# Moving norm, pooling and attention instructions within the full step of a fused conv and attention kernel

## The chip, the cores and the metric

The kernel runs on one core of one Trainium2 chip. The metric is the device time of one execution in microseconds (us). A core has five engines that run their own instruction queues strictly in program order and meet only at semaphores: TensorE (PE, matmuls into PSUM), VectorE (DVE), ScalarE (ACT), GpSimd (POOL, here mostly the issuer of DMAs that add in memory) and SyncE (SP, loads and stores).

## The reference

Eight images of 256 channels and 32x32 pixels pass through two residual blocks, each behind a group norm. The first is a pooling and convolution block, the second attention over the 1024 pixels.

```python
x = x + conv_block(_gn(x))
x = x + attention(_gn(x))

# conv_block: the stem, two chains of three 5x5 poolings each, four products
x_aux = silu(conv1x1(x, w_sta))
for _ in range(3):
    y1.append(0.9 * maxpool5(y1[-1]) + 0.1 * sumpool5(y1[-1]) / 25)   # the mixture
    y2.append(sumpool5(exp(y2[-1]) * y2[-1]) / (sumpool5(exp(y2[-1])) + 1e-6))
y = concat(silu(cv1(concat(y1))), silu(cv2(concat(y2))))       # 512 channels
a = c1(four depthwise 3-tap convolutions of y)
out = silu(cvend(y * a))

# attention: q = f w1, softmax(q f / 16) (f w2), without a key projection
```

## The kernel before

**Stages.** Phase a computes the stem, phase b the second pooling chain (`y2`) of all images into DRAM. Phase c, where the change lies, runs from 277 us to the end. It pipelines two images: step i does the convolution block of image i, the attention of image i-1, and the first pooling chain (`y1`, called "the chain") of image i+1. Steps 1 to 6 do all three (the full step; 1 to 5 are a hardware loop, which also loads for image i+2), step 0 has no attention, step 7 no chain, step 8 attention alone. The order on each engine is written out by hand in one function `step` for each engine, and nothing reorders it.

**Split products.** Each fp32 operand of a product is split in a high part (rounded, by ACT) and a low part (the rest, by DVE), and a product is three matmul passes: high by high, weights' low by high, weights' high by low. `product_split` walks the four 128-channel tiles k: tiles 0 to 2 in all three passes, then tile 3 in all three. Each output tile is 12 pairs of 512-column matmuls. The product cv1 takes the levels 0 to 3 of the chain; the last tile is level 3, the output of the third mixture. So of the first output tile of cv1, 9 pairs need levels 0 to 2 alone, pairs 10 and 11 need level 3's high part (`level_split_hi(act, i, LEVELS)`, L327) and pair 12 its low part (`level_split_lo(dve, i, LEVELS)`, L331).

**The chain.** Each level needs seven maxima on DVE (`maxima`, L309) and box sums made by eight DMA rounds (`add_round`), issued by POOL one after the other, each waiting for the one before. `mixture` (L318) joins both on DVE. `level_mixture(0)` stands in the attention's tile 2, `level_mixture(1)` behind the attention's last tile, and the third mixture (`mixture_of_added(dve, i, LEVELS - 1)`, output `last`) at the head of the next step. A mixture releases the DMA rounds of the next level.

**The norm of the attention.** At the end of a step DVE adds the block's output to x and takes statistics (`add_l0`, `bn_aggr`). At the head of the next step PE averages the means over groups in the middle of cv2's second output tile (L1313, `means`), DVE makes three small operations (L1602 to L1606), PE averages again (`variances`, between cv2 and cv1), DVE adds epsilon (L1616), POOL takes the power (L1173), DVE makes the shift (L1620), and ACT normalises (L1441) and splits (L1444).

**The head of a step.** ACT: high part of level 3, SiLU of the two cv2 tiles (L1384), centre taps 0 and 1 (L1391), the normalisation, further taps, SiLU of the cv1 tiles, then the products for q and v. DVE: outer taps (`outer_taps`, L1535, two instructions each, after their centre tap), `normalised_lo` (L1564), the low parts of q (L1650) and v (L1653). PE: cv2, variances, cv1, q products, v products, then the scores. `claim` makes PE wait until the PSUM slot of three uses ago is read.

**The attention tiles.** For each of eight query tiles t: PE score(t+1), turn_back(t-2), mix(t-1), turn(t) (a transpose of the exponentials); ACT the exponential (L1400), `turned_hi` (L1405), `scale_mixed` (L1419); DVE `turned_lo` (L1539), an outer tap, `maximum` (L1544), a piece of the chain, `invert`, `add_attention` (L1553). `inputs_lo` (L1560) follows. `released` gives the slots' conditions.

Of the kernel before, what the change touches and what calls it, by code (L numbers as in the profile page):

```python
# [38 lines left out]
KT = C4 // P  # L39
LEVELS = 3  # L40
# [946 lines left out]
MIX_AT = 2  # L987
# [6 lines left out]
def phase_c(nc, x, out, keep, levels, chain, pooled):  # L994

    with ExitStack() as ctx:
# [381 lines left out]
        def _(act):  # L1378
            def step(i, conv, attn, chained, ahead):
# [39 lines left out]
                    nc.scalar.activation(mixed[:, t % 2], ps_o[:, 0:C], ACT.Copy, scale=row_inv[:, t:t + 1]).then_inc(mixed_done.sem, 1)  # L1419

                slots_of = slot_plan(conv, attn)
                if conv and attn:
                    chain.level_split_hi(act, i, LEVELS)
                if conv and not attn:
                    for n, (c, s) in enumerate(schedule(attn)):
                        if s == 0:
                            silu_cv(c)
                        centre_tap(n)
                        if n == 1:
                            chain.begin_twos(act, i + 1, 1)  # L1430
                        if s == STAGES - 1 and c:
                            inputs_hi(c - 1)
                elif conv:
                    for n in range(CT):
                        silu_cv(n)
                    for n in range(CT):
                        centre_tap(n)
                if attn:
                    for t in range(CT):
                        wait(act, norm, i - 1, 6)  # L1440
                        nc.scalar.activation(a[:, t], x1[:, t], ACT.Identity, scale=rstd[:, t:t + 1],  # L1441
                                             bias=shift[:, t:t + 1]).then_inc(f_done.sem, 1)
                        wait(act, f_done, i - 1, t + 1)
                        nc.scalar.copy(f_hi[:, t], a[:, t]).then_inc(f_hi_done.sem, 1)  # L1444
# [19 lines left out]
                if attn:  # L1464
                    if conv:
                        centre_tap(BEFORE)
                    for t in range(TILES):
                        if t > 1:
                            scale_mixed(t - 2)
                        if t:  # L1470
                            turned_hi(t - 1)
                        if t == 1 and conv:
                            centre_tap(BEFORE + 1)
                        exponent(t)
                        if chained and t == MIX_AT + 1:
                            chain.begin_twos(act, i + 1, 1)
                        if t == TILES - 1:
                            turned_hi(t)
                        if conv and t and BEFORE + t + 1 < KT * STAGES:
                            centre_tap(BEFORE + t + 1)  # L1480
                    if conv:
                        inputs_hi(0)
                        inputs_hi(1)
                    scale_mixed(TILES - 2)
                    if conv:
                        inputs_hi(2)
                    scale_mixed(TILES - 1)
# [31 lines left out]
        def _(dve):  # L1519
            def step(i, conv, attn, chained, ahead):  # L1520
# [65 lines left out]
                def level_maxima(level, *at):  # L1586
                    chain.maxima(dve, i + 1, level, *at)
# [7 lines left out]
                before = iter(range(BEFORE if attn else KT * STAGES))  # L1595
                if conv and attn:
                    chain.level_split_lo(dve, i, LEVELS - 1)
                    chain.mixture_of_added(dve, i, LEVELS - 1)
                if attn:
                    small = Steps(dve, norm, i - 1)  # L1600
                    wait(dve, group_mean, i - 1, 1)
# [5 lines left out]
                if chained and not attn:  # L1607
                    chain.maxima(dve, i + 1, 0, first=chain.inner_ahead())
                if conv and attn:
                    chain.level_split_lo(dve, i, LEVELS)  # L1610
                elif conv:
                    outer_taps(next(before))
                    level_mixture(0)
# [8 lines left out]
                    outer_taps(next(before))  # L1622
                if conv and attn:
                    outer_taps(next(before))
                if attn:
                    for t in range(CT):
                        normalised_lo(t)
                        if conv:
                            outer_taps(next(before))
# [13 lines left out]
                if attn:  # L1643
# [14 lines left out]
                    for t in range(TILES):  # L1658
# [5 lines left out]
                            outer_taps(BEFORE + t)  # L1664
                        if t + 1 < TILES:
                            maximum(t + 1)
                        if chained and t == MIX_AT:
                            level_mixture(0)
                            level_maxima(1, 0, 1)
                        if chained and t > MIX_AT:  # L1670
                            level_maxima(1, t - MIX_AT + 1)
                        invert(t)
                        if t > 1:
                            add_attention(t - 2)
                    turned_lo(TILES - 1)
                    if conv:
                        for n in range(KT):
                            inputs_lo(n)
                if attn:
                    add_attention(TILES - 2)  # L1680
                if chained and not attn:
# [17 lines left out]
                else:  # L1699
# [28 lines left out]
                    if chained:  # L1728
# [2 lines left out]
                        level_maxima(2, 3, 4)  # L1731
                        for n in range(1, KT):
                            pooled.split_lo(dve, i + 1, n)
                        level_maxima(2, 5, 6)
                    if conv:
                        add_l0(0)
                if conv:
# [3 lines left out]
                    for m in range(CT):  # L1741
                        nc.vector.bn_aggr(mv[:, m, :], stats[:, m].rearrange("p h s -> p (h s)")).then_inc(bn.sem, 1)
                if chained:
                    chain.level_split_lo(dve, i + 1, 1)

            for n in range(KT):
# [44 lines left out]
```

## Time and profile before

| | |
|---|---|
| median of 3 runs | 1395.18 us (1388.47 to 1396.79) |
| the profiled execution | 1393.83 us, of which the span is 1391.9 us |
| PE, DVE, ACT, POOL busy | 87%, 83%, 52%, 22% of the span |
| instructions | 17764, 6702 of them matmuls |
| mean granted TensorE clock | 0.949 of full speed |
| DMA | 164.23 MB, 118 GB/s on average |

A share of the span is an average over phases with different limits. No engine is full, so the question at each stage is what its last wait was for. In the profile's chain of work that ended last, PE has 22% of the span, DVE 18%, DMA 16%, ACT 6%, and 17% is issue time without any shown wait.

### The profile page before, as it was taken

How to read it: one execution, taken by the hardware profiler on the slowest of the kernel's cores; microseconds unless marked ns; L12 is line 12 of the kernel's file. 1: busy time of each engine (PE TensorE's matmuls, PEld its weight loads, DVE VectorE, ACT ScalarE, POOL GpSimd, SP SyncE). 2: the span in 40 equal slices, each digit the busy share in tenths (PEclk: the TensorE clock that was granted, in tenths of full speed). 3: DMA queues.
4: the chain of work that ended last, by engine and by line, in shares of the span. 5: the costliest groups of instructions: out<-in, count | busy, mean ns of one | idle time of the engine just before them, and what ended most of it. 6: DMA issues, size and time to landing. Idle time of an engine off the chain costs nothing.

```text
span 1391.9 us, 17764 instructions
## 1 busy us (share of the span) xinstructions
PE 1213.2 (87%) x6702; PEld 1026.9 (74%) x6702; DVE 1154.5 (83%) x1220; ACT 723.2 (52%) x780; POOL 300.9 (22%) x256
## 2 busy tenths in 40 slices
PE   3569898675989999998999899999998999899697
PEld 1249898653768877877887788778887888788597
DVE  7779897599989989988998899889988986985443
ACT  1246766554366437634753566357545643754343
POOL 1567767501111111111111111111111111000000
PEclk9769998786999999999999999999999999999899
DMA  7403214544664576466646655764575457001000
GB/s 284 166 31 92 91 77 155 158 112 90 155 142 85 139 191 143 96 153 174 127 97 172 159 107 124 198 133 96 126 202 128 86 124 202 14 1 61 0 1 31
DMA packets 73310, 164.23 MB, mean 118 GB/s; under 512 B 33200, under 2 KB 35888, under 8 KB 73264
## 3 DMA queue, kind: packets, MB, share of 16 engines
q0 software_dynamic: 25200, 97.11, 31.1%
q1 hardware_dynamic: 47360, 66.20, 14.5%
q8 instruction: 31, 0.51, 0.2%
q10 hardware_dynamic: 704, 0.30, 0.1%
q14 instruction: 15, 0.12, 0.0%
HBM read 40.80 MB, written 25.17 MB: 47 GB/s over the span
## 4 chain that ended last, share of the span: by engine, by line
PE 22%; DVE 18%; issue 17%; DMA 16%; ACT 6%; DVEq 0%; POOL 0%; POOLq 0%; ACTq 0%
PE slot L1277 10%; DMA boxes<-twos 8%; PE ps_level L1277 8%; DMA twos<-boxes 5%; DVE between L1535 4%; DVE a L1535 4%; PE slot L1293 2%; DMA twos<-middle 2%; DVE pt_all L1539 2%; PE slot L1224 2%; ACT a L1441 1%; ACT between L1391 1%; DVE middle L318 1%; ACT y L1384 1%; DVE c_minus_max L1544 1%
## 5 line engine op out<-in xcount | busy, mean ns | idle before, releaser
L1277 PE MATMUL ps_level<-v_all,pt_all 128*128 128x256 f32 x1536 | 199.0, 286 | 13.0 <-DVE pt_all L1539 10.9
L1277 PEld LDWEIGHTS ps_level<-v_all,pt_all 128*128 128x128 f32 x1536 | 188.2, 191 | 18.3 <-DVE pt_all L1539 16.9
L1277 PE MATMUL slot<-f_all,q_all 128*128 128x512 f32 x768 | 189.7, 397 | 0.0
L1535 DVE SCALAR_TENSOR_TENSOR a<-between,k_columns,a 128x992 f32<-128x992 f32 (+1 forms) x128 | 157.6, 1232 | 6.9 <-ACT a L1391 4.6
L1277 PEld LDWEIGHTS slot<-f_all,q_all 128*128 128x128 f32 x768 | 140.1, 188 | 27.9
L1539 DVE TENSOR_TENSOR pt_all<-slot,pt_all 128x1024 fp32r<-128x1024 f32 x64 | 78.0, 1218 | 38.5 <-ACT pt_all L1405 38.2
L1419 ACT ACTIVATE mixed<-ps_level,row_inv 128x256 f32<-128x256 f32 x64 | 30.2, 472 | 133.9 <-PE ps_level L1277 133.9
L1391 ACT ACTIVATE a<-between,k_columns 128x1024 f32<-128x1024 f32 x64 | 79.3, 1239 | 33.6 <-DVE between L1535 32.6
L1414 ACT CAST v_all<-y 128x1024 fp32r<-128x1024 f32 x32 | 33.7, 1054 | 115.5 <-DVE y L1568 115.2
L1535 DVE SCALAR_TENSOR_TENSOR between<-y,k_columns,between 128x992 f32<-128x992 f32 x64 | 78.8, 1250 | 7.3 <-ACT between L1391 6.2
L1568 DVE SCALAR_TENSOR_TENSOR y<-slot,k_columns,y 128x1024 f32<-128x1024 f32 x32 | 40.9, 1283 | 52.2 <-PE slot L1224 50.6
L1405 ACT CAST pt_all<-slot 128x1024 fp32r<-128x1024 f32 x64 | 65.0, 1016 | 36.2 <-PE slot L1293 35.3
L1544 DVE TENSOR_REDUCE c_minus_max<-slot 128x1 f32<-128x1024 f32 x64 | 78.0, 1219 | 6.0 <-PE slot L1277 5.6
L1400 ACT ACTIVATE pooled<-slot,c_minus_max 128x1024 f32<-128x1024 f32 x64 | 71.6, 1119 | 21.8 <-DVE c_minus_max L1544 21.8
L1535 DVE SCALAR_TENSOR_TENSOR between<-a,k_columns,between 128x960 f32<-128x960 f32 x64 | 77.2, 1215 | 1.1
L1293 PE MATMUL slot<-k_ident,pooled 128*128 128x128 f32 x512 | 67.2, 274 | 10.2 <-ACT pooled L1400 10.2
L1224 PE MATMUL slot<-q_all,k_cv_hi 128*128 128x512 f32 x192 | 61.7, 425 | 12.0 <-ACT q_all L387 12.0
L853 POOL TENSOR_TENSOR e_lo<-x_all,e_hi 128x1024 fp32r<-128x1024 f32 x24 | 62.1, 2587 | 45.3 <-ACT e_hi L808 45.3
L1293 PEld LDWEIGHTS slot<-k_ident,pooled 128*128 128x128 f32 x512 | 56.8, 141 | 14.1 <-ACT pooled L1400 14.1
L1224 PE MATMUL slot<-f_all,k_c_hi 128*128 128x512 f32 x232 | 64.6, 400 | 0.4 <-DVE y L1568 0.4
L1224 PE MATMUL slot<-f_all,k_c_lo 128*128 128x512 f32 x232 | 63.5, 396 | 0.0
L1224 PE MATMUL slot<-q_all,k_c_hi 128*128 128x512 f32 x232 | 63.5, 395 | 0.0
(198 smaller groups left out, 2762.5 us busy)
## 6 DMA issues: line engine op xcount, KB each, us to landing
levels<-x_all SPq DMA_DIRECT2D x32, 512.0 KB, 2.6
boxes<-twos POOLq DMA_DIRECT2D x28, 543.0 KB, 4.7
boxes<-twos POOLq DMA_DIRECT2D x28, 527.0 KB, 4.6
x_all<-in_x SPq DMA_DIRECT2D x8, 1024.0 KB, 12.8
f_all<-levels SPq DMA_DIRECT2D x8, 1024.0 KB, 7.7
x<-in_x SPq DMA_DIRECT2D x8, 1024.0 KB, 6.1
out<-x SPq DMA_DIRECT2D x8, 1024.0 KB, 6.0
twos<-boxes POOLq DMA_DIRECT2D x14, 561.0 KB, 4.3
```

Source lines behind the costliest of these rows:

```text
L853: nc.gpsimd.tensor_tensor(e_lo[:, u], e[u], e_hi[:, u].bitcast(F32), ALU.subtract).then_inc(e_lo_done, 1)
L1224: last = nc.tensor.matmul(slot[:, hs], weights[:, k], inputs(k)[:, hs], start=(at == 0), stop=(at == len(uses) - 1))
L1277: last = nc.tensor.matmul(out, lhs, rhs, start=(n == 0), stop=(n == len(parts) - 1))
L1293: last = nc.tensor.transpose(slot[:, cols(m)], prob[:, cols(m)], keep["ident"][:, :])
L1391: nc.scalar.activation(dst, src, ACT.Identity, scale=keep["taps"][:, s, c, 1:2], bias=keep["b_taps"][:, s, c:c + 1]).then_inc(taps_centre. ...
L1400: nc.scalar.activation(prob[:, :], slots_of["s", t][:, :], ACT.Exp, bias=minus_max[:, t:t + 1], accum_out=row_sum[:, t:t + 1]).then_inc(pr ...
L1405: nc.scalar.copy(pt_hi[:, t % 2], slots_of["t", t][:, :]).then_inc(pt_hi_done.sem, 1)
L1414: nc.scalar.copy(y_hi[:, m], y[:, m]).then_inc(y_hi_done.sem, 1)
L1535: nc.vector.scalar_tensor_tensor(o, u, keep["taps"][:, s, c, tap:tap + 1], o, ALU.mult, ALU.add).then_inc(taps.sem, 1)
L1539: nc.vector.tensor_tensor(pt_lo[:, t % 2], slots_of["t", t][:, :], pt_hi[:, t % 2].bitcast(F32), ALU.subtract).then_inc(pt_lo_done.sem, 1)
L1544: nc.vector.tensor_reduce(minus_max[:, t:t + 1], slots_of["s", t][:, :], AX, ALU.max, negate=True).then_inc(maxed.sem, 1)
L1568: nc.vector.scalar_tensor_tensor(y[:, m], slots_of["c1", m][:, :], keep["b_c1"][:, m:m + 1], y[:, m], ALU.add, ALU.mult).then_inc(gated.se ...
```

## The change

Five pieces move, four of them in steps with attention and convolution; no instruction is added or removed.

1. DVE, head of the step: the third mixture goes behind norm's first three small operations; the low part of level 3 goes from there to behind the outer taps 0 and 1.
2. ACT, head of the step: the high part of level 3 goes behind the SiLU of both cv2 tiles and the centre taps 0 and 1.
3. ACT, attention's tile 7: its exponential goes ahead of `turned_hi(6)`. This holds for step 8 too.
4. DVE, attention's tiles: `invert` and `add_attention` go ahead of the chain's piece, and the last maximum of level 1 goes from tile 7 to between the third and the fourth `inputs_lo`.
5. DVE, tail of the step: the last two maxima of level 2 go behind the additions to x and the statistics.

```diff
@@ ScalarE
                 slots_of = slot_plan(conv, attn)
-                if conv and attn:
-                    chain.level_split_hi(act, i, LEVELS)
...
                     for n in range(CT):
                         centre_tap(n)
+                    chain.level_split_hi(act, i, LEVELS)
...
                             scale_mixed(t - 2)
+                        if t == TILES - 1:
+                            exponent(t)
                         if t:
                             turned_hi(t - 1)
...
-                        exponent(t)
+                        if t < TILES - 1:
+                            exponent(t)
@@ VectorE
                     chain.level_split_lo(dve, i, LEVELS - 1)
-                    chain.mixture_of_added(dve, i, LEVELS - 1)
...
                 if conv and attn:
-                    chain.level_split_lo(dve, i, LEVELS)
+                    chain.mixture_of_added(dve, i, LEVELS - 1)
...
                 if conv and attn:
                     outer_taps(next(before))
+                    chain.level_split_lo(dve, i, LEVELS)
...
+                        invert(t)
+                        if t > 1:
+                            add_attention(t - 2)
                         if chained and t == MIX_AT:
                             level_mixture(0)
                             level_maxima(1, 0, 1)
-                        if chained and t > MIX_AT:
+                        if chained and MIX_AT < t < TILES - 1:
                             level_maxima(1, t - MIX_AT + 1)
-                        invert(t)
-                        if t > 1:
-                            add_attention(t - 2)
                     turned_lo(TILES - 1)
                     if conv:
-                        for n in range(KT):
+                        for n in range(KT - 1):
                             inputs_lo(n)
+                    if chained:
+                        level_maxima(1, TILES - MIX_AT)
+                    if conv:
+                        inputs_lo(KT - 1)
...
-                        level_maxima(2, 5, 6)
...
                 if chained:
+                    if attn:
+                        level_maxima(2, 5, 6)
                     chain.level_split_lo(dve, i + 1, 1)
```

On VectorE at the head of the full step, before. L331 is a low part of a level, L318 the third mixture, L1602 to L1620 the norm, L1535 an outer tap; L95 and L81 prepare waits.

```order
L331 TENSOR_TENSOR pt_all<-middle,v_all 128x1024
L95 REGISTER_ALU
L81 ISA
L318 SCALAR_TENSOR_TENSOR last<-boxes,work_b 128x1024
L81 REGISTER_ALU
L1602 TENSOR_TENSOR c_dev<-c_mv,ps_level 128x2
L81 ISA
L1604 TENSOR_TENSOR c_dev<-c_dev 128x2
L81 REGISTER_ALU
L1606 TENSOR_TENSOR c_spread<-c_dev,c_mv 128x2
L95 REGISTER_ALU
L331 TENSOR_TENSOR pt_all<-last,v_all 128x1024
```

The same place after the change, from the third mixture on (the three small operations stand just ahead of it; L1537 is the outer tap's new line number).

```order
L318 SCALAR_TENSOR_TENSOR last<-boxes,work_b 128x1024
L81 REGISTER_ALU
L1617 TENSOR_SCALAR c_spread<-ps_level 128x2
L1618 TENSOR_SCALAR gmean<-ps_level 128x2
L81 REGISTER_ALU
L1621 TENSOR_TENSOR c_shift<-gmean,c_rstd 128x2
L95 ISA
L1537 SCALAR_TENSOR_TENSOR between<-y,k_columns,between 128x32x31
...
L331 TENSOR_TENSOR pt_all<-last,v_all 128x1024
L95 ISA
L1566 TENSOR_TENSOR f_all<-a,f_all 128x1024
```

Four outer-tap instructions (two outer taps, the last three replaced by the line of dots) now stand between the third mixture and level 3's low part, where there was none.

On ScalarE at the head of the full step, as one piece of the difference: L1384 is the SiLU of a cv2 tile, L1391 a centre tap, L327 the high part of level 3.

```order
+L1384 ACTIVATE y<-slot,k_columns 128x1024
+L95 REGISTER_ALU
+L1384 ACTIVATE y<-slot,k_columns 128x1024
+L1391 ACTIVATE between<-y,k_columns 128x1024 x2
+L95 ISA
 L327 CAST v_all<-last 128x1024
```

The four instructions that followed the high part of level 3 now precede it.

## Rows read from the trace of the kernel before

**Rows 1.** Chain of waits of 640 to 800 us: start us, us, what.

```profile
745.24 1.15 DVE middle L318
...
783.99 4.61 DMA boxes<-twos
...
788.73 1.24 DVE last L318
```

**Rows 2.** Timeline of DVE at the head of step 3: start us, us, instruction [idle before].

```profile
655.39 1.22 DVE L318 SCALAR_TENSOR_TENSOR last<-boxes,work_b 128x1024 f32<-128x1024 f32 x1 [1.66 <-DMA boxes<-twos]
...
660.87 4.99 DVE L1535 SCALAR_TENSOR_TENSOR between<-y,k_columns,between 128x992 f32<-128x992 f32 x4 [0.79 <-ACT between L1391]
665.78 1.22 DVE L1564 TENSOR_TENSOR f_all<-a,f_all 128x1024 fp32r<-128x1024 f32 x1
```

**Rows 3.** Timeline of ACT and of POOL at the same place.

```profile
659.61 2.37 ACT L1391 ACTIVATE between<-y,k_columns 128x1024 f32<-128x1024 f32 x2
...
656.67 0.55 POOL L214 DMA_DIRECT2D ahead_boxes<-ahead  x1
659.11 0.71 POOL L1173 TENSOR_TENSOR c_rstd<-c_spread,k_minus_half 128x2 f32<-128x2 f32 x1 [1.89 <-DVE gmean L1617]
```

**Rows 4.** Timeline of PE at the head of step 3, variances to the first score.

```profile
657.25 0.49 PE L1313 MATMUL ps_level<-c_spread,k_group 128*128 128x2 f32 x2 [2.87 <-DVE c_spread L1606]
...
664.72 0.63 PE L1224 MATMUL slot<-q_all,k_cv_hi 128*128 128x512 f32 x2
...
670.32 0.63 PE L1277 MATMUL slot<-f_all,k_w_hi 128*128 128x512 f32 x2
...
676.09 0.70 PE L1277 MATMUL slot<-k_w_hi,f_all 128*128 128x256 f32 x4
...
679.67 0.74 PE L1277 MATMUL slot<-k_w_hi,f_all 128*128 128x256 f32 x4 [0.55 <-DVE q_all L1650]
...
682.59 5.65 PE L1277 MATMUL slot<-f_all,q_all 128*128 128x512 f32 x24
```

**Rows 5.** Stretches of PE: length, busy (matmuls), granted clock, DMA share, GB/s.

```profile
657.60:661.92 4.32, 4.32 (x13) 0.63 0.73 258
332.13:337.20 5.07, 5.06 (x12) 0.56 0.55 106
343.96:348.13 4.17, 4.17 (x12) 0.66 0.00 0
```

**Rows 6.** Timeline of PE in step 0, two longer gaps.

```profile
332.13 2.93 PE L1264 MATMUL slot<-f_all,k_c_hi 128*128 128x512 f32 x6 [4.62 <-ACT f_all L1410]
...
343.96 2.93 PE L1264 MATMUL slot<-f_all,k_c_hi 128*128 128x512 f32 x6 [4.13 <-ACT f_all L1410]
```

**Rows 7.** Timeline of all engines in attention's tile 7 of step 3.

```profile
731.50 1.12 ACT L1400 ACTIVATE pooled<-slot,c_minus_max 128x1024 f32<-128x1024 f32 x1
731.63 1.23 DVE L1539 TENSOR_TENSOR pt_all<-slot,pt_all 128x1024 fp32r<-128x1024 f32 x1 [0.46 <-ACT pt_all L1405]
...
732.76 1.09 PE L1293 MATMUL slot<-k_ident,pooled 128*128 128x128 f32 x8 [1.03 <-ACT pooled L1400]
...
736.68 1.22 DVE L1539 TENSOR_TENSOR pt_all<-slot,pt_all 128x1024 fp32r<-128x1024 f32 x1
...
737.95 0.39 PE L1277 MATMUL ps_level<-v_all,pt_all 128*128 128x256 f32 x1 [1.24 <-DVE pt_all L1539]
```

**Rows 8.** Timeline of all engines, third mixture to first score in steps 1 and 7.

```profile
389.10 1.23 DVE L318 SCALAR_TENSOR_TENSOR last<-boxes,work_b 128x1024 f32<-128x1024 f32 x1 [0.58 <-DMA boxes<-twos]
...
391.19 0.28 PE L1313 MATMUL ps_level<-c_spread,k_group 128*128 128x2 f32 x2
...
416.33 0.86 PE L1277 MATMUL slot<-f_all,q_all 128*128 128x512 f32 x3
...
1186.45 1.22 DVE L318 SCALAR_TENSOR_TENSOR last<-boxes,work_b 128x1024 f32<-128x1024 f32 x1
...
1213.65 0.63 PE L1277 MATMUL slot<-f_all,q_all 128*128 128x512 f32 x2
```

## The prediction

> **What bounds the kernel now.** I read the chain of waits first. In steps 1 to 6 it runs through the third mixture, the DMA rounds of level 2 are the last thing before it, and they start from `level_mixture(1)`: 745.24 to 788.73 is 43.5 us, all DMA rounds and their issue [rows 1]. The mixtures stand 133.1 to 133.3 us apart, so the other 89.8 us (655.39 to 745.24) lead from one third mixture through the attention to `level_mixture(1)` [rows 1, 2]. Call the third mixture's start M. Nothing that merely happens earlier before M shortens a step, since M waits for the DMA (DVE idled 1.66 us for it) [rows 2]. Only work between M and `level_mixture(1)` counts.
>
> The timelines of each engine show what lies there. PE starts the first score at M + 27.20 in step 3 [rows 2, 4], and at M + 27.23 and M + 27.20 in steps 1 and 7, where PE's own waits and clock were different [rows 8]. A constant on such different PE timelines says that DVE set it: mixture, norm, outer taps, low parts of f and q, without a gap over 0.8 us. PE waited for DVE's q_lo (0.55 us) [rows 4]. From the first score on, DVE is busy without a gap until the tile-2 mixture is done, then PE is, until tile 7.
>
> **The change, part by part.** All times are those of step 3.
>
> Norm ahead of the mixture. DVE's three small operations go into its idle 1.66 us, the variances no longer wait, and PE's gap of 2.87 us with the slow stretch behind it goes [rows 4, 5]. ACT, freed of its wait for M, has SiLU and centre taps done before 657.2: two taps take 2.37 [rows 3], and cv2 ended before 654.4. Behind M (655.39 to 656.6) DVE adds epsilon; POOL is issuing DMAs until 657.22 and then takes the power, 0.71 [rows 3]; the shift ends at about 658.2, and the outer taps start at 658.3, not 660.87: 2.5 us earlier.
>
> The low part of level 3 is what this costs. It now follows those taps: 658.3 + 4.9 [rows 2] + 1.2 = 664.4, that is M + 9.0. Before, it ended at 658.9. PE starts cv1 2.8 us earlier, at 654.8, and has 11 of the first tile's 12 pairs to do before it needs that low part: 22 matmuls at 5.60/24 = 0.233 us (664.72 to 670.32 are 24) [rows 4] are 5.1 us, so it stands idle from 659.9 to 664.4, 4.5 us. The high part is ready in time (ACT at 657.9, needed at 659.0). PE's gap has moved and grown from 2.9 to 4.5 us.
>
> The clock. After the gap of 2.87 us 12 matmuls took 4.32 us at granted clocks down to 1.2 GHz, instead of 12 x 0.233 = 2.80: a loss of 1.5 us [rows 4, 5]. After gaps of 4.62 and 4.13 us, 12 took 5.07 and 4.17, losses of 2.3 and 1.4 [rows 5, 6]. The new gap is as long as these, so I take the fall for granted, at the 1.5 us of the same place, with 1.4 and 2.3 as ends.
>
> The Trainium skill (TensorE: Matmul & The Clock Gate, section Terms) puts the penalty at the throttled time times one minus the clock's ratio, half of it here. By that, the 4.32 us at a mean of 0.63 would lose 1.6 us, and the sum below would be 0.7 us larger over seven steps; the trace agrees within its rounding [rows 5].
>
> First score, new. 664.4, then 2 matmuls of cv1's first tile and 24 of the second (6.1), the clock's loss (1.5), 24 for q (5.6), two v products at 2.9 (679.67 to 682.59) [rows 4], 5.8: 683.4 = M + 28.0. DVE, 2 us ahead, no longer makes PE wait for f_lo or q_lo. Against 27.2 that is 0.8 us later: the bound passes from DVE to PE.
>
> Attention's tiles. In tile 2 the same DVE work lies before `turned_lo(2)` in either order, so PE's wait there stays. From tile 3 on PE sets the pace. In tile 7 the exponential starts at 730.6 instead of 731.50, and turn(7) about 0.9 earlier than 732.76 [rows 7]. But `turned_hi(6)` now follows it, and `turned_lo(6)` slips from 731.63 to about 732.7. Behind that DVE has an outer tap (2.4), `invert` and an addition (0.4); it no longer has a maximum (1.1). So `turned_lo(7)` starts at 732.7 + 1.1 + 2.4 + 0.4 = 736.6, where it started before, 736.68 [rows 7], and the last mix at 737.9 as before, 737.95. Gain: zero, given back within the tile. The maximum moved out fills DVE's 1.3 us wait ahead of the fourth `inputs_lo`, so it costs nothing; if that cover were gone, 1.1 us a step.
>
> Tail of the step. Statistics come 2.4 us earlier and PE's 0.9 us wait for the means goes. All of it is ahead of M: zero. DVE reaches the mixture at 654.4, still before the DMA (655.3). No queue gets a DMA earlier that could collide: the SP loads and the DMA rounds hang on c1, M and the mixtures, and shift with them. `level_mixture(0)` comes 0.6 us later, under the 4.4 us that level 1's DMA rounds have in hand before `level_mixture(1)`.
>
> **The sum.** Steps 2 to 6: 5 x 0.8 = 4.0. Step 1: PE's variances were late anyway, at 391.19 [rows 8], so SiLU, taps and low part end at 399.7; 399.7 + 6.1 + 1.5 + 5.6 + 5.8 = 418.7 against 416.33: 2.4. Step 7: DVE came to its mixture with no wait, so the small operations push M by 0.6 (1187.05), but POOL is free; low part at 1195.7, score at 1214.7 against 1213.65 [rows 8]: 1.0. In step 7's tile 7 no maximum leaves, so the slip of `turned_lo(6)` costs about 0.5, and in step 8, with nothing beside it, about 0.4 (estimates from the 0.9 to 1.0 slip, half of it covered by the earlier transpose). Together 8.3 us. The profiled execution takes 1393.83 us, which becomes 1402.1; the median of the three is 1.35 above it, and on that basis the forecast is **1403.5 us**, 0.6% slower. About 1% (14 us) is what a measurement of this kernel can tell from no change.
>
> **Rivals.**
> 1. The clock does not fall in the new gap, since PE is busy before it. For: gaps of 1.1 to 2.0 us show no fall. Against: 2.6 to 2.9 us did, in all of steps 2 to 6. It would take 7 x 1.5 = 10.5 off: 1393.0.
> 2. Slower by more: the clock falls early in the gap and stays low after it, as behind the 4.62 us gap, where the loss was 2.3 [rows 5, 6]. 7 x 0.8 = 5.6 more: 1409.1, just at the 1% bound. It decides from a slow stretch over 4.5 us behind the gap. For: the gap begins sooner, so the clock may already be down when work returns. Against: after 4.13 us it was 1.4.
> 3. Faster: DVE's lead passes through. DVE's taps and low parts from the second f_lo on run 2.0 us earlier (2.5 and 0.8 of ACT waits won, 1.15 for the moved low part lost; `normalised_lo` before at 665.78 [rows 2]). If cv1's first tile did not hold PE up, the first score would be at M + 25.2: 7 x 2.0 = 14 us, 1381. It needs PE to reach the v products by 673.8; against it stands the order of the passes, with pair 12 in the first tile.
> 4. The steps do not follow the first score, because DMA rounds, not the attention, set `level_mixture(1)`. Against: level 1's rounds end 4.4 us before it. The time would be the same: 1395.
>
> **How the numbers follow.** Forecast 0.58, rival 1 0.14, rival 2 0.14, rival 3 0.08, rival 4 0.06. Slower by over 1%: most of rival 2 and the forecast's upper edge, 0.14. Faster: rival 3, 0.07. Within 1%: 0.79. The range leaves out rival 3 and what exceeds rival 2: from rival 1 less 2 for its rounding, 1391, to 1410.
>
> **What would show it.** In the profile after: PE's wait at the variances under 1 us; a wait of about 4.5 us in the first cv1 tile, put down to DVE's low part of level 3 (`pt_all`, L331), and the slow clock behind it; no wait of PE for q_lo; the first score at M + 28.0; in tile 7 turn(7) earlier and the last mix where it was; mixtures 134.0 us apart. A gap under 4 us, or a first score before M + 27, would make the forecast wrong; so would a longer stretch from `level_mixture(1)` to M than 43.5.

## The result and the profile after

The changed kernel took 1396.91 us (median of 20 runs, 1394.2 to 1403.82), the kernel before 1393.53 us (20 runs): a ratio of 1.0032, interval 1.002 to 1.0045, or 4.5 us slower. The forecast was 1403.5 us, 8.3 us slower. Its range holds the time and its sign was right, but the cost came out at about half of it. One of the 20 runs of the kernel before took 4906.23 us and is left out of the ratio; the other 19 have a median of 1393.17 us. The profiled execution took 1402.05 us, almost exactly the 1402.1 forecast for it; that is luck, since it was the third slowest of the 20.

The step in which the forecast sees the cost looks as it said. Timeline of PE at the head of step 3 of the changed kernel, from the variances to the first score. The third mixture starts at M = 657.27.

```profile
656.45 0.38 PE L1313 MATMUL ps_level<-c_spread,k_group 128*128 128x2 f32 x2 [1.03 <-DVE c_spread L1607]
...
660.03 1.09 PE L1224 MATMUL slot<-pt_all,k_cv_hi 128*128 128x512 f32 x4
...
666.24 1.22 PE L1224 MATMUL slot<-pt_all,k_cv_hi 128*128 128x512 f32 x2 [4.18 <-DVE pt_all L331]
667.26 1.05 PE L1224 MATMUL slot<-q_all,k_cv_hi 128*128 128x512 f32 x2
...
675.11 0.63 PE L1277 MATMUL slot<-f_all,k_w_hi 128*128 128x512 f32 x2
...
680.71 0.64 PE L1277 MATMUL slot<-k_w_hi,f_all 128*128 128x256 f32 x4
...
686.32 4.06 PE L1277 MATMUL slot<-f_all,q_all 128*128 128x512 f32 x17
```

PE's gap at the variances is 1.03 us, where [rows 4] has 2.87. A gap of 4.18 us has come up in the first cv1 tile. There is no wait for q_lo (0.55 in [rows 4]). The score starts at M + 29.05 in this step, against 27.20. DVE and ACT at the same place:

```profile
657.27 1.23 DVE L318 SCALAR_TENSOR_TENSOR last<-boxes,work_b 128x1024 f32<-128x1024 f32 x1 [0.88 <-DMA boxes<-twos]
...
658.73 1.03 ACT L327 CAST v_all<-last 128x1024 fp32r<-128x1024 f32 x1
...
659.93 0.16 DVE L1621 TENSOR_TENSOR c_shift<-gmean,c_rstd 128x2 f32<-128x2 f32 x1 [1.18 <-POOL c_rstd L1173]
660.06 4.99 DVE L1537 SCALAR_TENSOR_TENSOR between<-y,k_columns,between 128x992 f32<-128x992 f32 x4
664.97 1.22 DVE L331 TENSOR_TENSOR pt_all<-last,v_all 128x1024 fp32r<-128x1024 f32 x1
...
679.17 1.23 DVE L1652 SCALAR_TENSOR_TENSOR q_all<-slot,q_all 128x1024 fp32r<-128x1024 f32 x1 [1.05 <-ACT q_all L1456]
```

The low part of level 3 ends at 666.2 = M + 8.9 (forecast M + 9.0): the gap ends with it. The high part starts at M + 1.5, in time. DVE now waits 1.05 us for q ahead of q_lo, where PE waited for q_lo before: the bound has passed to PE. In the view of all waits the new one is a row of its own (total us, times, longest):

```profile
PE slot L1224 <- DVE pt_all L331: 26.1, 7, 4.5
```

The clock behind the gap, as stretches of PE with the columns of [rows 5]: the first 12 matmuls in step 3, the next 4.88 us there (they reach 0.9 us into the q products), and the first 12 in step 5.

```profile
666.24:671.12 4.88, 4.88 (x12) 0.50 0.76 135
671.12:676.00 4.88, 4.88 (x20) 0.89 0.69 117
...
935.10:939.45 4.35, 4.35 (x12) 0.61 0.73 129
```

12 matmuls at full clock take 2.80 us. Step 5 lost 1.55 us, the forecast's figure. Step 3 lost 2.1 us and was still at a mean of 0.89 in the stretch after.

Tile 7 of step 3, all engines (score at 686.32):

```profile
735.58 1.09 PE L1293 MATMUL slot<-k_ident,pooled 128*128 128x128 f32 x8 [1.08 <-ACT pooled L1400]
736.46 1.22 DVE L1541 TENSOR_TENSOR pt_all<-slot,pt_all 128x1024 fp32r<-128x1024 f32 x1 [1.55 <-ACT pt_all L1405]
...
740.37 1.22 DVE L1541 TENSOR_TENSOR pt_all<-slot,pt_all 128x1024 fp32r<-128x1024 f32 x1
...
741.64 3.13 PE L1277 MATMUL ps_level<-v_all,pt_all 128*128 128x256 f32 x24 [0.77 <-DVE pt_all L1541]
```

Read each from its score, 682.59 before and 686.32 after. turn(7) is at +49.3, before at +50.2 [rows 7]: 0.9 earlier, as forecast. `turned_lo(6)` is at +50.1, before at +49.0: 1.1 later, as forecast. The last mix is at +55.3, before at +55.4: the zero, given back within the tile, as forecast. `level_mixture(1)` starts at 748.91 and the next third mixture at 792.09, 43.2 us later (43.5 in [rows 1]): still only DMA rounds. From step 1 to step 6 the mixtures stand 134.1 us apart on average (forecast 134.0, before 133.2, each between 133.0 and 133.3).

### The profile page after: what moved, and what is told of

Its sections match the earlier page's. It is cut to its first block, busy times and chain, and to the rows that moved or that the text cites. A ratio compares the mean times of both kernels' runs of the same rounds, so it can differ in the third digit from the quotient of the medians.

```text
span 1399.8 us, 17759 instructions
## 1 busy us (share of the span) xinstructions
PE 1211.9 (87%) x6702; PEld 1031.2 (74%) x6702; DVE 1150.6 (82%) x1220; ACT 727.0 (52%) x780; POOL 300.2 (21%) x256
## 4 chain that ended last, share of the span: by engine, by line
PE 29%; DMA 16%; issue 16%; DVE 16%; ACT 3%; POOL 1%; DVEq 0%; POOLq 0%; ACTq 0%
PE slot L1277 12%; DMA boxes<-twos 9%; PE ps_level L1277 7%; PE slot L1224 6%; DMA twos<-boxes 5%; DVE between L1537 4%; PE slot L1293 2%; DMA twos<-middle 2%; DVE a L1537 2%; DVE pt_all L1541 2%; DVE pt_all L331 1%; DVE c_minus_max L1546 1%; DVE middle L318 1%; DVE work_a L309 1%; PE slot L1264 1%
## 5 line engine op out<-in xcount | busy, mean ns | idle before, releaser
L1277 PEld LDWEIGHTS ps_level<-v_all,pt_all 128*128 128x128 f32 x1536 | 188.1, 191 | 26.1 <-DVE pt_all L1541 24.6
L1537 DVE SCALAR_TENSOR_TENSOR a<-between,k_columns,a 128x992 f32<-128x992 f32 (+1 forms) x128 | 157.5, 1231 | 3.1 <-ACT a L1391 0.8
L1391 ACT ACTIVATE a<-between,k_columns 128x1024 f32<-128x1024 f32 x64 | 79.3, 1238 | 33.5 <-DVE between L1537 32.8
L1400 ACT ACTIVATE pooled<-slot,c_minus_max 128x1024 f32<-128x1024 f32 x64 | 71.5, 1117 | 25.2 <-DVE c_minus_max L1546 21.8
L1570 DVE SCALAR_TENSOR_TENSOR y<-slot,k_columns,y 128x1024 f32<-128x1024 f32 x32 | 40.9, 1282 | 53.0 <-PE slot L1224 50.1
L1537 DVE SCALAR_TENSOR_TENSOR between<-y,k_columns,between 128x992 f32<-128x992 f32 x64 | 78.8, 1249 | 2.6 <-ACT between L1391 1.4
L1537 DVE SCALAR_TENSOR_TENSOR between<-a,k_columns,between 128x960 f32<-128x960 f32 x64 | 77.2, 1215 | 1.1
L1384 ACT ACTIVATE y<-slot,k_columns 128x1024 f32<-128x1024 f32 x32 | 35.5, 1111 | 69.2 <-PE slot L1224 69.2
```

Source lines behind the costliest of these rows:

```text
L1277: last = nc.tensor.matmul(out, lhs, rhs, start=(n == 0), stop=(n == len(parts) - 1))
L1384: nc.scalar.activation(y[:, c], slots_of["cv", k][:, :], ACT.Silu, bias=bias).then_inc(y_ready.sem, 1)
L1391: nc.scalar.activation(dst, src, ACT.Identity, scale=keep["taps"][:, s, c, 1:2], bias=keep["b_taps"][:, s, c:c + 1]).then_inc(taps_centre. ...
L1400: nc.scalar.activation(prob[:, :], slots_of["s", t][:, :], ACT.Exp, bias=minus_max[:, t:t + 1], accum_out=row_sum[:, t:t + 1]).then_inc(pr ...
L1537: nc.vector.scalar_tensor_tensor(o, u, keep["taps"][:, s, c, tap:tap + 1], o, ALU.mult, ALU.add).then_inc(taps.sem, 1)
L1570: nc.vector.scalar_tensor_tensor(y[:, m], slots_of["c1", m][:, :], keep["b_c1"][:, m:m + 1], y[:, m], ALU.add, ALU.mult).then_inc(gated.se ...
```

## The experiments

The first table gives what was timed, each against runs of the kernel before on the same chip. The second gives what the profiled execution of each shows. "M to score" sums the seven stretches from a third mixture to the first score, "rest" the remaining time from the first M to the end. "Low" is the time PE's clock stood at its lower level in steps 1 to 7, from M - 2 us to the score and in tile 7 (twice the sum of one minus the granted clock over stretches of 1 us).

| kernel | pieces | ratio (interval) | median us |
|---|---|---|---|
| before_again | none | 0.9994 (0.9977 to 1.0011) | 1393.0 |
| again | 1 to 5 | 1.0034 (1.0013 to 1.0056) | 1398.24 |
| head | 1, 2 | 1.0065 (1.004 to 1.009) | 1403.5 |
| rest | 3, 4, 5 | 1.0001 (0.9979 to 1.0023) | 1393.73 |
| head_tail | 1, 2, 5 | 1.0069 (1.0048 to 1.009) | 1402.57 |
| no_exp | 1, 2, 4, 5 | 1.0013 (0.999 to 1.0037) | 1395.09 |
| filler | 1 to 5, matmuls in the gap | 0.9995 (0.9974 to 1.0016) | 1392.7 |
| low_first | 1 to 5, low part ahead of the taps | 0.9905 (0.9882 to 0.9928) | 1381.75 |
| low_second | 1 to 5, low part between the taps | 0.9894 (0.9871 to 0.9918) | 1379.48 |
| low_first_no_exp | 1, 2, 4, 5, low part ahead | 0.9898 (0.9868 to 0.9927) | 1379.98 |
| head_low_first | 1, 2, low part ahead | 1.0006 (0.9985 to 1.0027) | 1393.96 |
| head_tail_low_first | 1, 2, 5, low part ahead | 0.9939 (0.9918 to 0.996) | 1385.58 |

| profile of | M to score | rest | low, head | low, tile 7 |
|---|---|---|---|---|
| before | 190.4 | 812.4 | 21.1 | 0 |
| before_again | 190.5 | 815.9 | 17.8 | 0 |
| after | 196.3 | 814.1 | 32.2 | 0 |
| again | 194.6 | 815.0 | 28.1 | 0 |
| head | 198.7 | 818.9 | 34.7 | 13.6 |
| rest | 190.4 | 816.3 | 24.6 | 3.4 |
| head_tail | 195.8 | 814.5 | 28.8 | 6.8 |
| no_exp | 192.9 | 812.3 | 21.4 | 0 |
| filler | 185.1 | 817.9 | 3.7 | 10.2 |
| low_first | 179.0 | 816.9 | 7.5 | 6.8 |
| low_second | 176.6 | 819.7 | 4.3 | 13.6 |
| low_first_no_exp | 180.0 | 813.0 | 11.3 | 6.8 |
| head_low_first | 186.5 | 820.6 | 21.0 | 13.6 |
| head_tail_low_first | 178.8 | 818.0 | 8.3 | 10.2 |

**The same two kernels once more.** `again` is the changed kernel, `before_again` the kernel before.

> The changed kernel once more, for a second profile beside the others. If the clock's loss behind the new gap differs from execution to execution, the distance from the third mixture to the first score differs from step to step again (25.9 to 29.2 us in the first profile) and in other steps than before, and the time is 0.2 to 0.5% over the kernel before. If the loss were fixed by the program, the same steps would show the same distances.

> The kernel before once more, for a second profile: what one execution differs by. 1.000. If the first profile was a lucky one behind step 1, this one shows more time between the third mixture of step 1 and the end than 1002.8 us (say 1005 to 1007), and perhaps a low clock in attention's tile 7 in some step, as the profile of pieces 3 to 5 alone showed in step 4. If it was a typical one: 1002 to 1004 us.

Measured 1.0034 and 0.9994. The size of the change stands, at half of the forecast. Of the kernel before, M to score is the same to 0.2 us in both profiles, while the rest differs by 3.5 us: single profiles can't settle less than that outside the head, and the forecast's profile was the luckier of the two.

**One part alone.**

```diff
 # head: pieces 1 and 2 of the change, 3 to 5 undone
 # rest: pieces 3 to 5 of the change, 1 and 2 undone
```

> Pieces 1 and 2 of the change alone (head of the step on VectorE and ScalarE). If the head makes the loss: slower than the kernel before by 0.2 to 0.5%, like the whole change, with PE's gap of 4 to 4.5 us at the low part of level 3 in cv1's first tile. If the loss comes from the other pieces: 1.000 or a gain.

> Pieces 3 to 5 alone (attention's tiles and the tail of the step). By my reckoning they give nothing in steps 1 to 6 and cost under 1 us in steps 7 and 8: 1.000 to 1.001. If the attention's additions ahead of the chain really buy PE time, 0.5 us or more a step: 0.997 or below. If they hold PE back: over 1.002.

Pieces 3 to 5 alone are a zero, 1.0001. All of the loss comes with the moved mixture and parts. That pieces 1 and 2 alone lose twice what the whole does was not expected (the intervals, 1.004 to 1.009 and 1.002 to 1.0045, overlap by little); the last experiments are about it.

**Matmuls in the gap.**

```diff
+                        if filler and at == len(uses) - 2:
+                            wait(pe, norm, i - 1, 5)
+                            for _ in range(26):
+                                nc.tensor.matmul(ps_o[:, C:HALF], w_hi[:, 0], keep["w1_hi"][:, 0], start=True, stop=True)
```

The wait in the first line holds these matmuls back until norm has read its sums from the same PSUM tile.

> The changed kernel with 26 matmuls of 256 columns, whose results nobody reads, on PE between pairs 11 and 12 of cv1's first tile (in steps with attention and convolution), about 3.0 us of work inside the gap of 2.8 to 4.5 us. If the loss behind the gap is the clock's, it goes: third mixture to first score 26.5 us in every step, and 4 to 10 us less than the changed kernel, 0.996 to 0.999 of the kernel before. If the loss is the wait itself and the clock does not matter: no change against the changed kernel, 1.003, or slower.

Timeline of PE in step 3 of this kernel, then two stretches of 2 us around the gap that is left (M = 650.69):

```profile
655.41 3.26 PE L1229 MATMUL ps_level<-k_w_hi,k_cv_hi 128*128 128x256 f32 x26
659.67 0.73 PE L1224 MATMUL slot<-pt_all,k_cv_hi 128*128 128x512 f32 x2 [1.00 <-DVE pt_all L331]
660.24 0.63 PE L1224 MATMUL slot<-q_all,k_cv_hi 128*128 128x512 f32 x2
```

```profile
658.00:660.00 2.00, 1.00 (x7) 1.00 0.58 109
660.00:662.00 2.00, 2.00 (x10) 1.00 0.17 27
```

The low part still comes at M + 9, but the clock stays up and the score starts at M + 26.36 in place of 27.55 to 29.17. That is the forecast's M + 28.0 without its 1.5 us for the clock, to 0.15 us. The loss of the change is gone (0.9995). The clock still fell, but elsewhere: the low time at the head went from 28 to 32 us down to 3.7 (all of it behind the long wait ahead of step 1's mixture), and 10.2 us came up in tile 7, where `after` and `again` have none.

**Without piece 3.**

```diff
-                        if t == TILES - 1:
-                            exponent(t)
...
-                        if t < TILES - 1:
-                            exponent(t)
+                        exponent(t)
```

> The changed kernel without piece 3: attention's last exponential stands behind turned_hi(6) again, as before the change. By my reckoning piece 3 gave back what piece 4 won in tile 7: turned_lo(6) starts 1 us earlier, the last mix at first score + 54.7 instead of + 55.3, 0.6 us a step, 4 to 5 us in all: 0.999 to 1.001 of the kernel before, against 1.003 with piece 3. If piece 3 is worth what it looks like (turn(7) 1 us earlier), this one is slower than the changed kernel: over 1.004.

Tile 7 of its step 3 (score at 679.97):

```profile
729.02 1.22 DVE L1538 TENSOR_TENSOR pt_all<-slot,pt_all 128x1024 fp32r<-128x1024 f32 x1 [0.46 <-ACT pt_all L1405]
...
730.15 1.09 PE L1293 MATMUL slot<-k_ident,pooled 128*128 128x128 f32 x8 [1.99 <-ACT pooled L1400]
...
732.93 1.21 DVE L1538 TENSOR_TENSOR pt_all<-slot,pt_all 128x1024 fp32r<-128x1024 f32 x1
...
734.77 3.11 PE L1277 MATMUL ps_level<-v_all,pt_all 128*128 128x256 f32 x24 [0.66 <-ACT mixed L1419]
```

turn(7) is back at +50.2, `turned_lo(6)` at +49.0, `turned_lo(7)` at +53.0 in place of +54.1, and the last mix at +54.8 in place of +55.3; `level_mixture(1)` follows 0.6 us earlier in each step. So piece 4 does win time, and piece 3 gives it back, as the forecast worked out. In the timed runs the two kernels (1.0034 and 1.0013) can't be told apart.

**The low part of level 3 earlier.** All five pieces stay; only DVE's low part moves, ahead of the outer taps (`low_first`) or between them (`low_second`).

```diff
+                if conv and attn:
+                    chain.level_split_lo(dve, i, LEVELS)    # low_first: here
                 if conv:
                     outer_taps(next(before))
                 if conv and attn:
+                    # low_second: here
                     outer_taps(next(before))
-                    chain.level_split_lo(dve, i, LEVELS)
```

> The changed kernel with one instruction back in front: the low part of level 3 right ahead of outer tap 0, behind norm's shift. If its place made the loss: PE's gap of 4 us at cv1's last pair is gone, PE comes to the q products at the third mixture + 10.8, waits for f_lo some 2 to 3 us there (at + 13.7), loses 0 to 1.5 us to the clock and starts the first score at + 25 to + 26.5: 1.5 to 2.5 us less a step than the changed kernel, 0.990 to 0.996 of the kernel before. If the taps' place matters more than the low part's: no gain against the changed kernel.

> The changed kernel with the low part of level 3 between outer taps 0 and 1, two tap instructions earlier than in the change and two later than in the run with the low part first. PE's gap at cv1's last pair should be 2.4 us shorter than in the change, 1.4 to 2.1 us, too short for the clock to fall in most steps, and made good by DVE being the bound again: first score at the third mixture + 25 to + 26, 0.990 to 0.994 of the kernel before. If the loss grew evenly with the low part's delay, it would lie half way between the change and the run with the low part first: 0.996 to 0.998.

DVE and PE in step 3 of `low_first`, M = 652.48:

```profile
655.28 1.23 DVE L331 TENSOR_TENSOR pt_all<-last,v_all 128x1024 fp32r<-128x1024 f32 x1
656.42 4.98 DVE L1537 SCALAR_TENSOR_TENSOR between<-y,k_columns,between 128x992 f32<-128x992 f32 x4
...
666.18 1.20 PE L1277 MATMUL slot<-f_all,k_w_hi 128*128 128x512 f32 x4 [2.35 <-DVE f_all L1566]
...
674.53 0.74 PE L1277 MATMUL slot<-k_w_hi,f_all 128*128 128x256 f32 x4 [0.55 <-DVE q_all L1653]
677.44 0.86 PE L1277 MATMUL slot<-f_all,q_all 128*128 128x512 f32 x3
```

The low part ends at M + 4.0. PE waits for it no more, but 2.35 us for f_lo and 0.55 for q_lo: DVE sets the score again, at M + 24.96, 2.2 us earlier than before the change. That is rival 3, which the forecast put at M + 25.2 and a gain of 14 us, to 1381; the gain was 12.4 us, from 1394.17 to 1381.75. Between the taps does as well. There PE's wait at the low part is 1.59 to 2.75 us in steps 2 to 6, and the clock never fell behind it. Both beat the kernel before by 1%.

**Both repairs.** As `low_first`, and without piece 3.

> Both repairs: the low part of level 3 ahead of the outer taps, and piece 3 left out. The two add up if they are independent: another 0.6 us a step below the run with the low part alone, 0.986 to 0.993 of the kernel before. If the DMA rounds of level 2 or the tail of the step bind instead, no more than the single repair.

0.9898, not to be told from 0.9905. The 0.6 us of tile 7 shows in four of the six full steps of its profile; in the other two the clock fell in that tile and the last mix came at + 56.3, where `low_first` without a fall has + 55.3. Rest is 813.0 against 816.9, though two profiles of one kernel differ by as much.

**Pieces 1 and 2 alone with the low part ahead of the taps.**

> The head of the step alone (pieces 1 and 2) with the low part ahead of the outer taps; attention's tiles and the tail as in the kernel before. If pieces 3 to 5 give nothing of their own: 0.989 to 0.993, like the run with all pieces. If the gain needs the earlier statistics of piece 5 (PE's wait for the means and then for the variances): 0.994 to 0.998.

1.0006: no gain, a surprise. ACT, DVE and PE in its step 3 (M = 656.28):

```profile
658.94 1.03 ACT L327 CAST v_all<-last 128x1024 fp32r<-128x1024 f32 x1
...
660.00 1.23 DVE L331 TENSOR_TENSOR pt_all<-last,v_all 128x1024 fp32r<-128x1024 f32 x1 [0.89 <-ACT v_all L327]
...
670.90 1.67 PE L1277 MATMUL slot<-f_all,k_w_hi 128*128 128x512 f32 x4 [2.35 <-DVE f_all L1563]
673.22 1.82 PE L1277 MATMUL slot<-f_all,k_w_hi 128*128 128x512 f32 x4
```

The high part comes at M + 2.66, in `low_first` at M + 1.26, so DVE waits 0.89 us for it. PE's wait for f_lo is the same 2.35 us as in step 3 of `low_first`, but here the clock falls behind it (four matmuls take 1.67 and 1.82 us, there 1.20 and 1.10), and in tile 7 of four steps too. In steps 3 to 7 of this kernel the wait is 2.35 or 2.36 us each time and the clock fell in all five; in steps 4 to 7 of `low_first` it is 1.63 to 1.94 us and the clock fell in none.

**Piece 5.** The last maxima behind the means, added to both kernels of pieces 1 and 2.

```diff
-                        level_maxima(2, 5, 6)
...
                 if chained:
+                    if attn:
+                        level_maxima(2, 5, 6)
                     chain.level_split_lo(dve, i + 1, 1)
```

> Pieces 1, 2 and 5, with the low part of level 3 ahead of the shifted row (outer tap 0). With pieces 1 and 2 alone this repair gave 1.0006, with the whole change 0.9905. Theory A: the missing third is piece 5: with it the high part of level 3 stands at M+1.3 to M+1.5, the low part at M+2.8, TensorE's wait of about 2 us for f_all falls at M+13.7 and the clock stays up from there to the score: M to score 24.9 to 25.5 in steps 2 to 6, ratio 0.989 to 0.993. Theory B (rival): it is the attention's part (piece 4, the additions ahead of the mixture) that TensorE's clock needs in tile 7, and the head has the high part at M+1.4 but the clock still falls behind it, M to score 26 to 26.6, and the ratio stays at 0.998 to 1.002.

> Pieces 1, 2 and 5 of the change, without 3 and 4. Both theories price the gap alike; they differ in what piece 5 (the last maxima behind the means) is worth once the head of a step no longer has the two mixtures in front of it. Theory A: pieces 1 and 2 alone measured 1.0065 and the whole 1.0034 because without piece 5 the means reach TensorE about 1 us later against the third mixture M (its wait for c_mv at M-3.6 in place of c_spread at M-0.9), so ScalarE's high part of level 3 starts at M+2.5 instead of M+1.45, while M itself gains nothing. Then this kernel stands with the whole change or below it: high part at M+1.4 to M+1.5, gap 3.8 to 4.5, M to score 27.8 to 28.2 in most steps, ratio 1.001 to 1.0035. Theory B (rival): the difference between the two was the granted clock's doing (low for 6.8 us instead of 3.4 in three steps, and low in tile 7 in four), which piece 5 has no hand in: then the high part's place changes and the ratio stays at 1.005 to 1.008.

With the low part ahead, piece 5 is what was missing at the head: high part at M + 1.3 to M + 1.6 in steps 2 to 6, M to score 24.85 to 25.60, the sum 7.7 us down, the median 8.4 us down. ACT and PE of its step 3 (M = 654.52):

```profile
656.14 1.03 ACT L327 CAST v_all<-last 128x1024 fp32r<-128x1024 f32 x1
...
668.20 1.20 PE L1277 MATMUL slot<-f_all,k_w_hi 128*128 128x512 f32 x4 [1.72 <-DVE f_all L1563]
669.71 1.09 PE L1277 MATMUL slot<-f_all,k_w_hi 128*128 128x512 f32 x4
```

The ratio, 0.9939, stayed a little above theory A's 0.993. With the low part late, the high part moved about as expected (M + 1.3 to M + 1.9), and so did gap and score, but the time didn't: 1.0069, as for `head`, and inside theory B's range. Theory A falls there. It is piece 4 that parts 1.0069 from `no_exp`'s 1.0013 (the intervals don't meet; the two were timed on different chips, each against the kernel before on its own), and likewise 0.9939 from 0.9898 (these do). Of that 0.56%, 7.5 us, the profiles show the 0.6 us a step in tile 7, 3.7 us over steps 1 to 6. In tile 7 of two steps of `head_tail` the clock also fell, in none of `no_exp`. Stretches of 1 us from step 4 of `head_tail` (columns as above):

```profile
867.77:868.77 1.00, 0.26 (x2) 1.00 0.00 0
868.77:869.77 1.00, 0.15 (x2) 1.00 0.24 46
869.77:870.77 1.00, 0.82 (x7) 0.90 1.08 215
870.77:871.77 1.00, 1.00 (x6) 0.50 1.07 207
871.77:872.77 1.00, 1.00 (x7) 0.50 0.65 113
872.77:873.77 1.00, 1.00 (x7) 0.50 0.73 229
```

The last mix of that step stood at its score + 56.3, not + 55.3. All four kernels with pieces 1 and 2 but not 4 had such falls, in 13 of 28 steps; the eight profiles with piece 4 had them in 12 of 56, the two of the kernel before in none of 14. In step 8, which these counts leave out, one profile of the kernel before (`before_again`) has such a fall too. One profile each doesn't tell a habit of a kernel from chance.

## Why the prediction was right in direction and too large

**The bound and the place: right.** M to the first score, set by DVE before, by PE after; no other stretch moved by more than two profiles of one kernel differ. That DVE set the score before shows in steps 5 and 6 of `before_again`: there the clock did not fall, and the score stood at M + 27.2 all the same. Rival 4 is out: `low_first` moved the score by 2.2 us in steps 3 to 6 and the kernel by 1%.

**The moved low part: right.** M + 8.9 against M + 9.0, a gap of 3.84 to 4.51 us in steps 2 to 6 against 4.5. (The forecast called a gap under 4 us a sign of being wrong; step 6, with 3.84, is the one such gap in `after` and `again`.) That this is the cause, and not something beside it, is shown by `low_first` and `low_second`, which move that one instruction and turn 1.0034 into 0.9905 and 0.9894.

**The clock in steps 2 to 6: right, at the low end.** After gaps of 3.69 to 4.88 us the clock fell in all 25 steps of the five profiles that have them (after, again, head, head_tail, no_exp), and in 7 of the 25 it stayed low twice as long. Score at M + 28.3 on average in `after`, M + 28.0 in `again`; forecast M + 28.0. The term was 4.0 us and measured 5.6 and 3.9. Rival 1 was out (`filler` shows what it would have been: 0.9995), and rival 2 happened in a quarter of the steps.

**Steps 1 and 7: the part that failed.** The forecast gave them 2.4 and 1.0 us, and both hold the same 1.5 us of clock loss behind the low part. It had not worked out the gap in these two steps. It is 2.39 to 2.89 us, not 4.5, and behind it the clock fell in 2 of 5 profiles in step 1 and in 3 of 5 in step 7. The gap's length alone would not have put this right: rival 1 is turned down because gaps of 2.6 to 2.9 us had cost the clock in all of steps 2 to 6. That reading came from one profile. In the second one of the same kernel gaps of 2.53 and 2.81 us cost the clock and one of 2.71 us did not (step 5 of `before_again`). In step 7, the gap in PE's timeline and the clock of the 12 to 13 matmuls behind it; first the changed kernel's profile,

```profile
1202.36 0.73 PE L1224 MATMUL slot<-pt_all,k_cv_hi 128*128 128x512 f32 x2 [2.82 <-DVE pt_all L331]
```

```profile
1202.45:1205.35 2.90, 2.90 (x13) 1.00 0.00 0
```

and the same place in `again`:

```profile
1195.53 0.73 PE L1224 MATMUL slot<-pt_all,k_cv_hi 128*128 128x512 f32 x2 [2.82 <-DVE pt_all L331]
```

```profile
1195.60:1199.75 4.15, 4.15 (x12) 0.59 0.00 0
```

The same gap of 2.82 us, once without and once with the fall. With it the score starts at M + 27.48 (forecast M + 27.65), without it at M + 25.94, earlier than the 27.20 before the change. From M to the score, step 1 measured + 1.6 and 0.0, step 7 - 1.3 and + 0.3 in `after` and `again`. With the 0.5 us by which step 7's mixture is pushed (forecast 0.6), the two steps cost 0.8 us on average, where the sum had 3.4.

Step 1 had a second error. The forecast kept its variances "late anyway", at M + 2.09 as before, and so had the low part end at M + 10.6. Step 1 of the changed kernel (M = 389.35), the variances and the pair behind the low part:

```profile
390.63 0.42 PE L1313 MATMUL ps_level<-c_spread,k_group 128*128 128x2 f32 x2
...
399.32 1.22 PE L1224 MATMUL slot<-pt_all,k_cv_hi 128*128 128x512 f32 x2 [2.39 <-DVE pt_all L331]
```

The variances stand at M + 1.28 (`again` M + 1.17), the low part ends at M + 9.9 and 9.8. In `head`, which lacks piece 5, they are at M + 2.10 and M + 10.7; in `head_tail`, which differs from it by piece 5 alone, at M + 0.44 and M + 9.0. So piece 5 was not all "ahead of M": as far as single profiles show it, its earlier statistics made step 1's low part 0.7 us earlier than forecast.

**The sum.** From the first M to the end the two profiles of the changed kernel take 1010.4 and 1009.6 us, the two of before 1002.8 and 1006.4: 5.4 us more on average, of which steps 2 to 6 are 4.7 (forecast 4.0), steps 1 and 7 are 0.8 (3.4), and the rest 0 (0.9 for the tiles 7 of steps 7 and 8). The timed runs say 4.5 to 4.7. So the term that was mis-sized is that of steps 1 and 7: 2.6 us too many. Of these, 1.5 us are the clock loss, forecast for both steps and there in one of the two in each profile; 0.7 are the place of step 1's low part; the rest is in small pieces. A few longer slow stretches in steps 2 to 6 gave 0.7 back. The two small estimates for tile 7 hold where they can be seen: the last mix of step 7 is at its score + 54.5, before at + 53.9 (forecast 0.5), that of step 8 at + 54.0, before at + 53.5 where the clock did not fall (forecast 0.4). In the rest of the span they are lost among the 3.5 us by which two profiles of one kernel differ there. The time itself also stood on a base that was too high: 1395.18 us, the median of three runs, where 20 have 1393.53. Of the 6.6 us between 1403.5 and 1396.91, 1.65 are that base.

**Tile 7, tail: right,** zero each in the steps where the forecast had zero (`rest` at 1.0001, and the last mix at + 55.3), but for piece 5 in step 1, as said above. The reason, piece 3 giving back what piece 4 wins, is shown by the profile of `no_exp` and was not resolved by its time.

**Open.** Why the kernels without piece 4 lose 3 to 4 us more in the timed runs than their tile 7 explains. Over the 20 runs of the changed kernel, time goes with the mean granted clock of the run: the six fastest took 1395.1 us on average at 0.9517, the six slowest 1401.6 at 0.9463. The six runs of `head_tail` had a median clock of 0.9425, the twelve of `no_exp`, which differs by piece 4 alone, 0.9475. So the difference goes with the clock, but one profile of `head_tail` doesn't show where: its 1010.4 us from the first M is that of the changed kernel. That piece 4 itself keeps the clock up is not shown. The Trainium skill (TensorE: Matmul & The Clock Gate, Terms) prices throttled time at half of it here. By that, 0.001 of mean clock would cost an estimated 1.4 us; the 20 runs give 6.5 us for 0.0054, 1.2 us for 0.001, near it.

## What to carry to other kernels

When an instruction is moved down an in-order queue, ask for every product it leaves behind which matmul of the consumer needs it, and in which step; here a 1.2 us operation behind 5 us of others turned a 1% gain into a 0.3% loss, and moving it up by two instructions gave the gain back. Work out the gap for each kind of step before a clock loss is put behind it, and read the falls from more than one profile: a gap of 3.7 us and more cost the clock every time, one of 2.4 to 2.9 us in 12 of 19 cases, and to take that for certain was more than half of what the failed term had too much. An order that wins on one engine can be undone by its neighbour (pieces 4 and 3), so try the pieces apart before the set is judged.

## What was not expected of the hardware

- PE's clock fell in 25 of 25 steps behind gaps of 3.69 to 4.88 us ahead of level 3's low part and in 5 of 10 behind gaps of 2.39 to 2.89 us, and the same gap of 2.82 us gave both. All waits of PE over 1.5 us between M and the score, in all 14 profiles, by their length, with a fall in the wait or in the 2.5 us behind it: 1.59 to 2.12 us, in 2 of 20; 2.25 to 2.36 us, in 8 of 14; 2.39 to 2.89 us, in 12 of 19; 3.69 to 5.48 us, in 31 of 31.
- It fell in tile 7 too, in 25 steps, in 20 of which no single wait there is over 1.3 us (1.99 in the others). In step 4 of `head_tail` PE had been busy for 0.26 and 0.15 of two successive microseconds before. It did not fall in every step that has the same waits.
- 26 matmuls that nothing reads, put in the gap, kept the clock up there and cost nothing, since PE had no work: the pair behind them still waited 0.74 to 1.30 us for the low part.
- The time before the change's first step varied between executions of nearly the same program by 7.5 us: the first third mixture stood between 382.17 (`head`) and 389.68 us (`head_tail`), before the change in 389.10 and 386.97. Spans alone hide effects of this size; the stretch from a fixed instruction doesn't.
